# Expert attention: where DVE adds the fc2 bias, before or after a row's closing steps

## The chip, the cores and the metric

The kernel runs on one NeuronCore of a Trainium2 chip. Its time is the device time of one execution, in microseconds, and of several runs the median is compared. The engines are TensorE (PE; its weight loads are PEld), VectorE (DVE), ScalarE (ACT), GpSimd (POOL) and SyncE (SP), which only issues DMAs.

## The reference

The reference is a small audio network: a strided depthwise convolution, an ALiBi attention, the expert attention of this change, a Taylor-series attention and a mixture of experts. `h` has 32 batch rows of 188 positions and 64 channels. The part that matters (NH = 4 heads, NE = 4 query sets, called experts, D = 16):

```python
sx = einsum("bsh,ndh->bnsd", x, hl_w) + hl_b
q, k, v = per expert and head, per head, per head          # from sx
att = softmax(causal(q @ k.T * d ** 0.5))                  # one for each head and expert
qkv = where(pad, 0, att @ v)                               # "the mask"
gs = softmax(gate logits of qkv)                           # over the experts
hn = layernorm(sum over experts of qkv * gs + resid)
fx = hn by heads
hx = relu(where(fx == 0, 0, fx @ fc1_w.T + fc1_b))
hx = where(fx == 0, 0, hx @ fc2_w.T + fc2_b)               # "+ fc2_b" is the step that moves
fout = layernorm(hx + fx)
fg = softmax(fout @ fgate_w.T)
h = h + fout * fg                                          # "the closing steps"
```

## The kernel before, in words

The activations of all rows stay in SBUF, in the tensor `stream`; weights lie in `wsb`. `expert_attention` (from line 778) works as a software pipeline with one turn for each batch row. Each of the four engines runs its own `body(t, par)`, written out by hand, and in turn `t` each works on eight rows at once, at lags 0 to 7: LN, FRONT, UNIT, TAIL, NORM, MLP, FIN and LAST. In the code of a turn `rf`, `ru`, `rt`, `rz`, `rm`, `rn` and `rl` are these rows. `skewed_loop` (line 1452) writes out the first turns (the pipeline fills), loops over pairs of turns, and writes out the last ones (it drains, turns 32 to 38). The order on each engine is the order of the code. Waits between engines are semaphores named after the tile.

TensorE splits a turn into four steps `e`, one for each query set. In each it does the scores of that set (L1064, L1067, into PSUM banks `T`), the shifted queries of the next (L1041 to L1046), the maxima scores two sets ahead (L1028 to L1035, into `R`) and the weighing of the values of the set before (L1081, L1085, into `O`). Between these stand 14 small products, all of which use one PSUM bank, `X`, in the fixed order of the list `FILLS` (all at L993). Each must wait until the engine that reads the one before has said `..._used`:

```python
FILLS = [("znT", MLP), ("fg", LAST), ("sx", FRONT),
         ("pickA", TAIL), ("kb01", FRONT), ("kb23", FRONT), ("q01", FRONT),
         ("pickB", TAIL), ("fc1", MLP), ("k", FRONT),
         ("q23", FRONT), ("v", FRONT), ("xT", LN), ("fc2", MLP)]
```

`fc2` is the last product of a turn (behind the weighing of step 3). The next turn starts with the scores of set 0, and then come the transposes `znT`, which overwrite `X` and so wait for `fc2_used`. That semaphore is set by DVE's `hx = X + fc2_b` (L1376). After `znT` follow queries, `fg` (the gate product, read by DVE at L1281 and L1282, which frees the bank), maxima scores, the weighing of set 3, `sx`, and in step 1 the scores, `pickA`, queries and `kb01`. `pickA` waits for ACT's copies `sxT` and `sxb` (L1159). ACT overwrites `sxT` only after DVE's mask of set 3 of the row two before (`need(act, sem["o_used"], ...)`). `kb01` waits for DVE's `outs` (L1264).

DVE's turn begins with the sum over the experts (L1274, which waits for POOL's `mixed`, L967), the MLP's mask (L1277), the gate's maximum (L1281, L1282), additions to `z` (L1289, L1291), the maxima of set 2 (L1245, L1248) and the mask of set 3 (L1254). It ends with the maxima of set 1 of the next row, the gate of the experts (L1360 to L1362), the mask of set 2 (L1254), then the closing steps of row `rl` (L1368, L1369, L1370, L1371, L1373: sum, reciprocal, the gate, the product, the addition to `stream`; each waits for the one before through `link`), and last the bias of row `rm` (L1376). The closing steps exist in turns 7 to 38 and the bias in turns 5 to 36. POOL computes `mixed` (two instructions) at the turn's end, then zeroes the part above the diagonal of the exponentials (L979). In the first turns TensorE has one extra group of 16 matmuls per entry of `WARM_AT`, the last of them in turn 6 (just ahead of the stretch from 676 us that the rows below show).

Of the kernel before, what the change touches and what calls it, by code (L numbers as in the profile page):

```python
# [20 lines left out]
ALU = mybir.AluOpType  # L21
# [3 lines left out]
B, T_IN, C = 32, 375, 64  # L25
# [3 lines left out]
P = N // 2  # L29
HALVES = 2  # L30
# [335 lines left out]
class Steps:  # L366
# [12 lines left out]
    def link(self, ins):  # L379
        self.mark(ins)  # L380
        self.settle()
# [396 lines left out]
def expert_attention(env):  # L778
# [14 lines left out]
    with ExitStack() as ctx:  # L793
        def sb(name, shape, dt=F32):
            return ctx.enter_context(nc.sbuf_tensor("ex_" + name, shape, dt))
# [4 lines left out]
        def psum(name, shape):  # L800
            return ctx.enter_context(nc.psum_tensor("ex_" + name, shape, F32))
# [43 lines left out]
        hx = sb("hx", [P, HALVES, C])  # L845
# [8 lines left out]
        X = psum("X", [128, 512])  # L854
# [6 lines left out]
        sem = {n: ctx.enter_context(nc.semaphore("ex_" + n)) for n in names}  # L861
# [4 lines left out]
        def valid(r):  # L866
            return not isinstance(r, int) or 0 <= r < B

        def row_halves(r):
            return stream[:, bass.ds(r * HALVES, HALVES), :]  # L870

        def over_halves(name):
            return w(name, P).unsqueeze(1).broadcast_to([P, HALVES, w(name, P).shape[1]])

        def heads(t):

            return t.rearrange("p h (n d) -> p h n d", n=NH)
# [349 lines left out]
        def _(dve):  # L1227
            steps = Steps(dve, sem["dve_step"])
            link = steps.link
            tt, ts, red = nc.vector.tensor_tensor, nc.vector.tensor_scalar, nc.vector.tensor_reduce  # L1230
# [20 lines left out]
            def mask_values(r, e, par):  # L1251

                dve.wait_ge(sem["o_full"], r * NE + e + 1)
                nc.vector.scalar_tensor_tensor(oT[par][:, e, :], sxT[par][:, 0:N], 0.0, O[:, 0:N], ALU.not_equal,  # L1254
                                               ALU.mult).then_inc(sem["o_used"], 1)
# [11 lines left out]
            def body(t, par):  # L1267
                rf, ru, rt, rz, rm, rn, rl = (t - lag for lag in (FRONT, UNIT, TAIL, NORM, MLP, FIN, LAST))
# [94 lines left out]
                       top[:].unsqueeze(2).broadcast_to([P, HALVES * NH, NE]), ALU.mult).then_inc(sem["gs_ready"], 1)  # L1363
                if valid(ru):
                    mask_values(ru, 2, par)
                if valid(rl):
                    dve.wait_ge(sem["fexp_ready"], rl + 1)
                    link(red(fsum[:], fexp[:], AX.X, ALU.add))  # L1368
                    link(nc.vector.reciprocal(fsum[:], fsum[:]))  # L1369
                    link(tt(fexp[:], fexp[:], fsum[:].unsqueeze(2).broadcast_to([P, HALVES, NH]), ALU.mult))  # L1370
                    link(tt(heads(fout[:]), heads(zn[odd][:, :, 1, :]), fexp[:].unsqueeze(3)  # L1371
                            .broadcast_to([P, HALVES, NH, D]), ALU.mult))
                    link(tt(row_halves(rl), row_halves(rl), fout[:], ALU.add))  # L1373
                if valid(rm):
                    dve.wait_ge(sem["fc2_full"], rm + 1)
                    tt(hx[:], X[0:P, 0:HALVES * C].rearrange("p (h c) -> p h c", h=HALVES), over_halves("fc2_b"), ALU.add)\  # L1376
                        .then_inc(sem["fc2_used"], 1)

            dve.wait_ge(sem["consts"], CONSTS)
            skewed_loop(dve, body, DEPTH, steps, 2 * STEPS)  # L1380


# [812 lines left out]
```

## Time and profile before

| | us |
|---|---|
| median of 3 runs | 2023.95 (2016.03 to 2024.33) |
| the profiled execution, its own time | 2016.92 |
| its span, first to last instruction | 2015.0 |
| busy in the span: TensorE / its weight loads | 1701.8 / 1243.2 |
| busy in the span: DVE / ACT / POOL | 1382.7 / 768.3 / 595.6 |
| mean granted TensorE clock | 0.795 |

Times are microseconds from the start of the span. A row of a timeline is a run of like instructions: start, length, engine, line, operation, what it writes and reads, the shape, how many, and in brackets how long the engine stood idle before it and for whom. The ends of matmuls are modelled. The granted clock is a share of full speed: 1.00 is 2.4 GHz, 0.50 is 1.2 GHz. The page's chain of waits covers only the end of the program here.

### The profile page before, as it was taken

Reading aid. Unit: us, or ns where it says so; the run is one execution under the profiler, and the core shown is the slowest. Engines: PE = TensorE matmul, PEld = TensorE weight load, DVE = VectorE, ACT = ScalarE, POOL = GpSimd, SP = SyncE. Lnnn points to the kernel's source line nnn. Section 1 sums busy time; section 2 is a strip of 40 time slices with the busy share of each in tenths; the row PEclk is TensorE's granted clock in tenths of the full one; section 3 lists DMA queues with packets and bytes.
Section 4 is the critical chain, followed back from the end, with each engine's and each line's share of the span. In section 5 each row is a group of like instructions: output and inputs, shape, how many; then the busy total and the mean of one; then the engine's idle time right before and its main releaser. Section 6 shows DMA issues by size and latency. Waiting matters only on the chain. (4 is left out here: it accounts for less than half of the span.)

```text
span 2015.0 us, 45178 instructions
## 1 busy us (share of the span) xinstructions
PE 1701.8 (84%) x15237; PEld 1243.2 (62%) x15240; DVE 1382.7 (69%) x4295; ACT 768.3 (38%) x2210; POOL 595.6 (30%) x906
## 2 busy tenths in 40 slices
PE   1499999999769899999999999962999999788897
PEld 1266666666535556565555555541888888677776
DVE  6276766666527777777777777774766665688887
ACT  2255444454334444444444444421222222344443
POOL 2522222222134433333333333332211211322221
PEclk9999999999879977777777777765555555687888
DMA  2000000000000000000000000000000000000000
GB/s 114 1 2 0 0 0 0 0 0 0 1 1 2 2 1 0 0 0 0 0 0 0 0 0 0 0 1 0 1 0 0 0 0 1 1 5 6 5 4 13
DMA packets 6978, 8.12 MB, mean 4 GB/s; under 512 B 6272, under 2 KB 6272, under 8 KB 6784
## 3 DMA queue, kind: packets, MB, share of 16 engines
q1 hardware_dynamic: 6912, 7.25, 1.1%
q8 instruction: 40, 0.66, 0.1%
q14 instruction: 26, 0.21, 0.0%
HBM read 5.71 MB, written 1.54 MB: 4 GB/s over the span
## 5 line engine op out<-in xcount | busy, mean ns | idle before, releaser
L604 ACT ACTIVATE al_prob<-al_S,al_negmax 94x94 f32<-94x94 f32 (+1 forms) x512 | 145.9, 376 | 176.2 <-DVE al_negmax L731 176.1
L979 POOL TENSOR_SCALAR_AFFINE_SELECT ex_pT<-ex_pT 128x512 f32<-128x512 f32 (+1 forms) x256 | 129.3, 528 | 246.6 <-ACT ex_pT L1196 195.1
L505 PE MATMUL al_S<-al_kpad,al_qT 128*94 128x376 f32 x384 | 163.0, 507 | 0.0
L1245 DVE TENSOR_REDUCE ex_negmaxA<-ex_R 128x4 bf16<-128x512 f32 x128 | 88.9, 694 | 80.4 <-PE ex_R L1029 78.7
L682 POOL TENSOR_TENSOR al_kpad<-al_kT,al_quad_mask 128x1504 f32<-128x1504 f32 x32 | 86.2, 2694 | 183.7 <-ACTq L619 183.7
L731 DVE TENSOR_REDUCE al_negmax<-al_S 94x2 f32<-94x376 f32 (+1 forms) x192 | 99.2, 542 | 58.4 <-PE al_S L506 52.5
L1595 POOL TENSOR_TENSOR ta_kk<-ta_ext 94x320 f32<-94x320 f32 x64 | 60.4, 962 | 246.2 <-DVE ta_qkn L1775 166.1
L961 POOL TENSOR_TENSOR ex_zrstd<-ex_zvar,neg_half 94x16 f32<-94x16 f32 x34 | 98.6, 2901 | 77.1 <-DVE ex_zvar L1320 77.1
L1170 ACT ACTIVATE ex_pT<-ex_T 128x496 f32<-128x496 f32 x128 | 74.8, 584 | 92.8 <-PE ex_T L1067 92.7
L741 DVE RECIPROCAL al_rec<-al_O 128x188 f32<-128x188 f32 x64 | 84.9, 1327 | 32.1 <-PE al_O L543 32.1
L2004 ACT ACTIVATE mo_hT<-mo_H,wsb 128x188 f32<-128x188 f32 x256 | 88.4, 416 | 38.8 <-PE mo_H L1964 36.2
L1964 PE MATMUL mo_H<-mo_xT,w_parts 128*128 128x188 bf16 x768 | 93.7, 283 | 9.2 <-ACT mo_hT L2004 9.2
L1940 PE MATMUL mo_Y<-wsb,mo_hT 128*94 128x64 f32 x1024 | 100.4, 261 | 0.0
L1940 PEld LDWEIGHTS mo_Y<-wsb,mo_hT 128*94 128x94 f32 x1024 | 97.3, 177 | 0.3 <-issue 0.2
L993 PE MATMUL ex_X<-ident,ex_zn 94*128 94x94 f32 x136 | 32.5, 381 | 71.1 <-DVE ex_hx L1376 63.6
L1064 PE MATMUL ex_T<-ex_qm,ex_kT 32*128 32x188 f32 x1024 | 90.8, 417 | 0.9
L1964 PEld LDWEIGHTS mo_H<-mo_xT,w_parts 128*128 128x128 bf16 x768 | 73.3, 113 | 22.3 <-ACT mo_hT L2004 20.8
L1041 PE MATMUL ex_T<-ex_sxT,wsb 128*128 128x188 f32 x256 | 84.4, 419 | 0.0
L505 PEld LDWEIGHTS al_S<-al_kpad,al_qT 128*94 128x94 f32 x384 | 59.3, 168 | 39.1 <-issue 38.7
L993 PE MATMUL ex_X<-wsb,ex_oT 128*94 128x84 f32 x512 | 76.8, 311 | 5.2 <-ACT ex_sxb L1159 3.7
L737 DVE COPY al_probT<-al_PT 94x752 f32<-94x752 f32 x64 | 59.5, 930 | 29.5 <-PE al_PT L523 29.5
L967 POOL TENSOR_TENSOR ex_mixed<-ex_outs,ex_gate 94x256 f32<-94x256 f32 x64 | 39.5, 636 | 136.1 <-DVE ex_gate L1362 136.1
(321 smaller groups left out, 4471.2 us busy)
## 6 DMA issues: line engine op xcount, KB each, us to landing
tok_xin<-x_t SPq DMA_DIRECT2D x4, 760.0 KB, 7.2
wsb<-weights SPq DMA_DIRECT2D x1, 2531.0 KB, 13.9
out<-stream SPq DMA_DIRECT2D x16, 94.0 KB
tok_par<-tok_w SPq DMA_DIRECT2D x1, 4.5 KB, 1.6
```

The source lines that it names most:

```text
L505: nc.tensor.matmul(S[0:P, k, 0:2 * N], q, s, start=True, stop=False)
L604: last = nc.scalar.activation(p[:, k, cols], S[0:P, k, cols], ACT.Exp, bias=negmax[g % 2][:, m:m + 1])
L682: nc.gpsimd.tensor_tensor(kpad[par][:].rearrange("p j g n -> p j (g n)"), kT[:].rearrange("p g n -> p (g n)").unsqueeze(1).broadcast_to([1 ...
L731: nc.vector.tensor_reduce(dst, src, AX.X, ALU.max, negate=True).then_inc(max_done, 1)
L961: nc.gpsimd.tensor_tensor(zrstd[:], zvar[:], neg_half[0:P, 0:HALVES * 2 * NH], ALU.pow)\
L979: nc.gpsimd.affine_select(out=view, in_=view, compare_op=ALU.is_ge, fill=0.0, base=shift, pattern=[[0, NH], [1, cols]], channel_multiplier ...
L993: last = nc.tensor.matmul(dst, a, m, start=True, stop=True)
L1064: last = nc.tensor.matmul(T[:, n, 0:N], kT[par][rows, 0:K0], qm[e % 2][rows, :], start=True, stop=True, tile_position=(32 * n, 0), skip_gr ...
L1245: red(negmaxA[e % 2][:, D::32], R[:, 0, :].rearrange("p (n s) -> p n s", n=NH), AX.X, ALU.max, negate=True)\
L1940: last = nc.tensor.matmul(YB[h][0:P, e * C:(e + 1) * C], hT[p][:, e, h * P:(h + 1) * P], w("w2")[:, e * C:(e + 1) * C], start=True, stop=True)
L1964: last = nc.tensor.matmul(HB[e // 2 % 2][:, (e % 2) * N:(e % 2 + 1) * N], w_parts[:, b, e * HID:(e + 1) * HID], xT[p][:, a, :], start=(n = ...
L2004: nc.scalar.activation(hT[p][:, e, :], HB[e // 2 % 2][:, (e % 2) * N:(e % 2 + 1) * N], ACT.Gelu, bias=w("b1")[:, e:e + 1]).then_inc(h_read ...
```

## The change

On DVE, the block with the wait for `fc2_full` and the bias goes from the end of the turn to just behind the mask of set 2. Nothing else is changed: the same instructions, semaphores and operands.

```diff
                 if valid(ru):
                     mask_values(ru, 2, par)
+                if valid(rm):
+                    dve.wait_ge(sem["fc2_full"], rm + 1)
+                    tt(hx[:], X[0:P, 0:HALVES * C].rearrange("p (h c) -> p h c", h=HALVES), over_halves("fc2_b"), ALU.add)\
+                        .then_inc(sem["fc2_used"], 1)
                 if valid(rl):
                     dve.wait_ge(sem["fexp_ready"], rl + 1)
                     link(red(fsum[:], fexp[:], AX.X, ALU.add))
                     link(nc.vector.reciprocal(fsum[:], fsum[:]))
                     link(tt(fexp[:], fexp[:], fsum[:].unsqueeze(2).broadcast_to([P, HALVES, NH]), ALU.mult))
                     link(tt(heads(fout[:]), heads(zn[odd][:, :, 1, :]), fexp[:].unsqueeze(3)
                             .broadcast_to([P, HALVES, NH, D]), ALU.mult))
                     link(tt(row_halves(rl), row_halves(rl), fout[:], ALU.add))
-                if valid(rm):
-                    dve.wait_ge(sem["fc2_full"], rm + 1)
-                    tt(hx[:], X[0:P, 0:HALVES * C].rearrange("p (h c) -> p h c", h=HALVES), over_halves("fc2_b"), ALU.add)\
-                        .then_inc(sem["fc2_used"], 1)
```

## Rows read from the trace of the kernel before

**Rows 1.** The page's slices of the span (50.4 us each): TensorE's granted clock, in tenths

```profile
PEclk9999999999879977777777777765555555687888
```

**Rows 2.** Waits of the stage, 566 to 1392 us: in total, times, longest

```profile
PE ex_X L993 <- DVE ex_hx L1376: 63.6, 30, 4.9
```

**Rows 3.** DVE's timeline, one steady row: start, length, line, [idle before]

```profile
1019.30 0.15 DVE L1368 TENSOR_REDUCE ex_fsum<-ex_fexp 94x2 f32<-94x8 f32 x1
...
1019.68 0.76 DVE L1370 TENSOR_TENSOR ex_fexp<-ex_fexp,ex_fsum 94x8 f32<-94x8 f32 x1
...
1021.64 0.29 DVE L1376 TENSOR_TENSOR ex_hx<-ex_X,wsb 94x128 f32<-94x128 f32 x1
```

**Rows 4.** TensorE's timeline, the same row

```profile
1018.90 0.54 PE L993 MATMUL ex_X<-wsb,ex_h1m 64*94 64x64 f32 x4
...
1022.08 0.65 PE L993 MATMUL ex_X<-ident,ex_zn 94*128 94x94 f32 x4 [1.92 <-DVE ex_hx L1376]
...
1023.81 0.59 PE L1028 MATMUL ex_R<-ex_kpadb,ex_qTb 128*128 128x512 bf16 x1
...
1026.56 0.99 PE L993 MATMUL ex_X<-ex_xT,wsb 64*128 64x188 f32 x2
...
1028.75 1.57 PE L993 MATMUL ex_X<-wsb,ex_oT 128*94 128x84 f32 x8
```

**Rows 5.** Stretches: length, each engine's busy time, granted clock, DMA share, GB/s

```profile
677.10:696.91 19.81, 17.62 (x218) 11.64 (x218) 15.98 (x49) 10.09 (x26) 8.84 (x14) 1.00 0.01 2
...
724.74:1318.63 593.89, 536.92 (x5228) 349.33 (x5228) 432.14 (x1290) 245.17 (x623) 215.52 (x310) 0.78 0.00 0
...
995.63:1009.28 13.65, 12.70 (x82) 7.91 (x82) 8.05 (x24) 4.24 (x11) 3.14 (x7) 0.50 0.00 0
...
1022.92:1033.16 10.24, 10.05 (x67) 6.04 (x66) 5.52 (x20) 3.67 (x10) 2.07 (x5) 0.50 0.00 0
...
193.49:196.91 3.42, 3.42 (x8) 1.54 (x7) 1.12 (x3) 1.54 (x7) 0.00 (x0) 0.50 0.00 0
```

**Rows 6.** TensorE's timeline, turns 6 and 7, at full clock

```profile
679.15 0.38 PE L1028 MATMUL ex_R<-ex_kpadb,ex_qTb 128*128 128x512 bf16 x1
...
680.81 0.58 PE L993 MATMUL ex_X<-ex_xT,wsb 64*128 64x188 f32 x2
...
683.29 0.87 PE L993 MATMUL ex_X<-wsb,ex_oT 128*94 128x84 f32 x8 [1.19 <-ACT ex_sxb L1159]
...
685.25 0.32 PE L993 MATMUL ex_X<-ex_sxb,ex_ewkb 128*128 128x188 bf16 x2 [0.63 <-DVE ex_outs L1264]
...
699.55 0.74 PE L993 MATMUL ex_X<-ident,ex_zn 94*128 94x94 f32 x2 [1.84 <-DVE ex_hx L1376]
```

**Rows 7.** DVE's timeline, turns 6 and 7

```profile
676.71 0.34 DVE L1254 SCALAR_TENSOR_TENSOR ex_oT<-ex_sxT,ex_O 128x188 f32<-128x188 f32 x1
...
677.10 0.29 DVE L1376 TENSOR_TENSOR ex_hx<-ex_X,wsb 94x128 f32<-94x128 f32 x1
...
678.14 1.12 DVE L1274 TENSOR_REDUCE ex_z<-ex_mixed 94x64 f32<-94x256 f32 x2 [0.76 <-POOL ex_mixed L967]
...
681.99 0.33 DVE L1254 SCALAR_TENSOR_TENSOR ex_oT<-ex_sxT,ex_O 128x188 f32<-128x188 f32 x1
...
696.65 0.34 DVE L1254 SCALAR_TENSOR_TENSOR ex_oT<-ex_sxT,ex_O 128x188 f32<-128x188 f32 x1
```

**Rows 8.** ACT's timeline, turn 7

```profile
682.42 0.42 ACT L1159 ACTIVATE ex_sxT<-ex_X,wsb 128x188 f32<-128x188 f32 x1 [2.74 <-DVE ex_oT L1254]
```

**Rows 9.** POOL's timeline, the steady row of rows 3

```profile
1019.18 1.24 POOL L967 TENSOR_TENSOR ex_mixed<-ex_outs,ex_gate 94x256 f32<-94x256 f32 x2 [4.10 <-DVE ex_gate L1362]
```

**Rows 10.** The bias in the steady rows: durations, first and last start

```profile
L1376 DVE TENSOR_TENSOR ex_hx<-ex_X,wsb x25: 286/286/288, 724.7 to 1318.6; 94x128 f32<-94x128 f32 x25
```

**Rows 11.** DVE's timeline, a draining turn

```profile
1366.96 0.16 DVE L1370 TENSOR_TENSOR ex_fexp<-ex_fexp,ex_fsum 94x8 f32<-94x8 f32 x1
...
1370.62 0.16 DVE L1281 TENSOR_REDUCE ex_ftop<-ex_X 94x2 f32<-94x8 f32 x1 [2.21 <-PE ex_X L993]
```

## The prediction

> **What bounds the kernel now.** I read the page first, for where the time lies and what clock it had; then the waits of the stage of the expert attention, for what TensorE waits on; then the timelines of TensorE and DVE across one steady row; then the same two timelines across the one row that ran at full clock without closing steps; last the stretches with their granted clock.
>
> The expert attention's rows run from about 566 to 1392 us. TensorE's granted clock has a 9 in the two slices from 604 to 705 and a 7 in every one of the twelve behind them, the steady rows [rows 1]. The largest wait of TensorE in the stage is for `hx`, the very instruction that the change moves: 63.6 us in 30 rows, 2.1 each, one in each turn in which both a bias and closing steps exist (turns 7 to 36) [rows 2]. In the steady row shown, DVE starts the first closing step at 1019.30, right behind the row's last mask. L1370 alone takes 0.76. The bias starts at 1021.64, so the closing steps hold it back by 2.34 us [rows 3]. The matmul that it reads (fc2) ended at 1018.90 + 0.54 = 1019.44. TensorE, which runs in order, ends its scores about 1020.15 and stands idle for 1.92 us until the transposes of `zn` can overwrite `X` at 1022.08 [rows 4]. So the bias could have run from about 1019.5 to 1019.8, before TensorE wanted the bank.
>
> The second reading is the clock. It fell to 0.50 (1.2 GHz) at 1022.92, behind that gap, and was back at 1.00 (2.4 GHz) at 1033.16; the stretch before, from 995.63 to 1009.28, was the same thing one row earlier. Over the 24 steady periods the mean is 0.78, so 0.44 of the time, 10.9 us of a row, runs at half clock [rows 5]. At half clock the maxima matmuls and the weighing, up to the start of `sx`, take 1023.81 to 1026.56 = 2.75 us [rows 4]; at full clock the same matmuls take 679.15 to 680.81 = 1.66 us [rows 6]. A microsecond of gapless work at half clock is thus 0.60 of one at full clock and loses 0.40.
>
> **The change, step by step.** No instruction is added or removed, and none issues a DMA. On DVE the 0.29 us bias with its wait for fc2 goes ahead of five closing steps. No queue of POOL, ACT or SP is reordered.
>
> *Gap at znT.* Gone at both clocks: TensorE reaches the transposes about 0.35 us after the bias could end. In turn 6, where there are no closing steps, the mask starts at 676.71, the bias at 677.10 [rows 7], and TensorE never waited between scores and transposes. Nearest bounds for the new wait for fc2, behind which the closing steps are now queued: 0 (turn 6) to the 0.14 by which fc2's end at 1019.44 lies behind 1019.30 [rows 3, 4]; I take 0.1.
>
> *What is late next.* The closing steps still stand before the next turn's work on DVE, and its mask of the last query set (L1254) gates ACT's copies of `sxT` and `sxb`, then `pickA`, then `kb01`. Turn 6 into 7 shows that chain at full clock: the mask starts at 681.99, ACT waited 2.74 us for it and starts at 682.42 [rows 7, 8]; `pickA` starts at 683.29 after TensorE idled 1.19, `kb01` at 685.25 after 0.63 more for `outs` [rows 6]. From there TensorE is dense until the next fc2. That turn's whole period, mask to mask, is 696.65 - 676.71 = 19.94 us at clock 1.00 [rows 5, 7]. Adding closing steps in its place behind the bias moves the mask. Raw, they are 2.34 long; 0.76 of that falls into DVE's wait for POOL's `mixed` at 678.14 [rows 7], plus some 0.1 of wait for fc2: 19.94 + 1.6 = 21.5. But L1370 is not 0.76 long by itself. Without POOL beside it, it is 0.16 [rows 11]; in the steady row it ends at 1019.68 + 0.76 = 1020.44, just as `mixed` ends at 1019.18 + 1.24 = 1020.42 [rows 3, 9]. Started 0.4 later it should end at the same moment, so I take off the 0.4 that bias and wait cost: a mask 1.1 later, a period of **21.05 us** at full clock. Bounds 20.4 (closing steps shrink to their unheld length) and 21.6 (none of it absorbed).
>
> *The clock.* The idle piece at `pickA` grows from 1.19 to 1.19 + 1.1 = 2.3 us, longer than the 1.92 behind which the clock falls now; 1.19 with 0.63 behind it did not bring it down [rows 5, 6]. So I expect the clock to fall still, but at `pickA`, and to return sooner: in the steady row it was back at 1033.16, 4.4 us after `pickA` began at 1028.75 [rows 4, 5], because then the wide matmuls run. The shortest low stretch in the trace is 3.42 [rows 5], the longest 13.65. I take 4.5 us of low work, 0.40 x 4.5 = 1.8, in 8 rows of 10, since a gap of 2.3 sits near the boundary between what did and did not bring it down: 1.45 a row. Period 21.05 + 1.45 = **22.5**.
>
> The Trainium skill's page "TensorE: Matmul & The Clock Gate", section "HAM oscillation — how this bites in real kernels", prices throttled time at half of it, 1 - 1.2/2.4. By that the 4.5 us would cost 2.25, not 1.8, a row 22.85 and the whole 8 us more. No row here shows a full 0.5; the pair above measures 0.40 with its weight loads and small matmuls, and the measurement decides.
>
> *Sum.* Steady period now: (1318.6 - 724.7)/24 = 24.745 [rows 10]. 24 x (24.745 - 22.5) = 53.9. Turn 7 has one idle piece of 1.84 at the same place [rows 6]: 1.8. In the draining turns 33 to 36 TensorE has little to do and the chain bias, transposes, `fg`, L1281 is serial; DVE idles up to 2.21 at L1281 [rows 11], so 0 to 2.2 each, I take 1.25: 5. Together **61 us**. The profiled execution took 2016.92 (span 2015.0 and 1.9 around it), so 1956 on its scale; the median of the runs is 2023.95, 7 above it, and the forecast is made against that: **1963**.
>
> **The rivals.**
> - *The clock holds.* For it: two slices of this stage (604 to 705 us) have a 9 for the clock, in turns with gaps of 1.19 and 0.63 [rows 1, 6]. Against: the new gap is longer than the one that brings it down now. Period 21.05, 24 x 3.695 + 7 = 96 us less: **1928**.
> - *The clock falls at `pickA` and returns later*, after 7 us of low work: the row has 21.05 + 2.8 = 23.85; 24 x 0.9 + 7 = 28 less: **1996**. For it: the remaining wait at `kb01` still thins the work right behind.
> - *Slower: the low stretch keeps its length and lands on the dense part.* Now half of it lies between transposes and `kb01`, where TensorE has 1.19 + 0.63 = 1.8 us of slack at full clock anyway [rows 6]. From `pickA` on it has none. With stretches of 10.24 and 13.65 as now (mean 11.9) [rows 5], a row is 21.05 + 4.8 = 25.8, 24 x 1.06 - 7 = 18 more: **2042**. It turns from gain to loss at a low stretch of (24.745 + 0.29 - 21.05)/0.40 = 10 us. Against it: the return 4.4 us behind `pickA`.
> - *No difference:* the same stretch at 9 to 11 us, or fc2 so late that the closing steps lose what TensorE gains; within 10 us of **2024**.
>
> **How the numbers follow.** Forecast 0.52, clock holds 0.20, later return 0.15, no difference 0.06, slower 0.07. Two in ten may lie outside; 1925 to 2000 takes in the first three with their bounds (a period of 20.4 would reach 1913, unlikely). Faster by over 0.5% (10 us, about what a measurement of this kernel can tell): the first three, 0.87.
>
> **What would show it.** In the changed profile the row "TensorE waits for `hx`" should be nearly gone; L1254 and then the bias stand back to back, with L1370 shorter than 0.76; a wait of TensorE at `pickA` for ACT's `sxb` of about 2 us a row should be new; ACT's `sxT` should wait for `oT`. The mean clock of the steady rows should be 0.88 to 0.95. The forecast is wrong if the clock stays at 0.78 or lower, or is 1.00 throughout, or if the bias idles for fc2 by more than 0.3 us a row.

## The result, and the profile after

The changed kernel takes 1943.22 us (median of 4 runs, 1939.4 to 1945.91), the kernel before 2021.39 us (4 runs, 2016.03 to 2024.33). The ratio is 0.9615, 95% interval 0.9586 to 0.9644: 78 us faster. The forecast was 1963, with a range of 1925 to 2000. The profiled execution has a span of 1937.5 us, against 2015.0. Its page, busy time of three engines and TensorE's clock by slices (now 48.4 us each):

```profile
PE 1621.5 (84%) x15237; PEld 1186.3 (61%) x15240; DVE 1358.8 (70%) x4295; ACT 765.0 (39%) x2210; POOL 595.3 (31%) x906
...
PEclk9999999999969998889888888855555555897888
```

The same instructions ran. The slices of the steady rows had a 7 before [rows 1] and have mostly an 8 now. TensorE's busy time fell by 80 us with the same 15237 matmuls: they were shorter, not fewer. The waits of the stage (in total, times, longest), 566 to 1320 us:

```profile
ACT ex_sxT L1159 <- DVE ex_oT L1254: 95.1, 29, 3.6
...
PE ex_X L993 <- ACT ex_sxb L1159: 39.6, 31, 1.5
...
PE ex_X L993 <- DVE ex_hx L1368: 9.5, 4, 3.6
```

The wait for the bias, 63.6 us in 30 rows before [rows 2], is 9.5 us in 4 rows, all of them where the pipeline drains. In its place stands TensorE's wait for ACT's `sxb`, 1.3 us a row; ACT in turn waits for DVE's mask of set 3, 3.60 us in the row shown. That row on DVE, from the end of turn 21 into turn 22 (the counterpart of rows 3 and 7; `hx` is now at L1368 and the closing steps at L1372 to L1377):

```profile
1002.58 0.35 DVE L1254 SCALAR_TENSOR_TENSOR ex_oT<-ex_sxT,ex_O 128x188 f32<-128x188 f32 x1
...
1003.02 0.29 DVE L1368 TENSOR_TENSOR ex_hx<-ex_X,wsb 94x128 f32<-94x128 f32 x1
...
1003.60 0.37 DVE L1374 TENSOR_TENSOR ex_fexp<-ex_fexp,ex_fsum 94x8 f32<-94x8 f32 x1
...
1004.01 0.68 DVE L1375 TENSOR_TENSOR ex_fout<-ex_zn,ex_fexp 94x128 f32<-94x128 f32 x1
...
1005.68 1.12 DVE L1274 TENSOR_REDUCE ex_z<-ex_mixed 94x64 f32<-94x256 f32 x2 [0.55 <-DVE stream L1377]
...
1007.51 0.29 DVE L1289 TENSOR_TENSOR ex_z<-ex_z,residual 94x128 f32<-94x128 f32 x1 [0.15 <-DVE ex_fgate L1282]
...
1007.72 0.28 DVE L1291 TENSOR_TENSOR ex_z<-ex_hx,ex_zn 94x128 f32<-94x128 f32 x1
...
1008.98 0.34 DVE L1254 SCALAR_TENSOR_TENSOR ex_oT<-ex_sxT,ex_O 128x188 f32<-128x188 f32 x1
```

And on TensorE, the same row (the counterpart of rows 4 and 6):

```profile
1002.44 0.54 PE L993 MATMUL ex_X<-wsb,ex_h1m 64*94 64x64 f32 x4
...
1003.83 0.68 PE L993 MATMUL ex_X<-ident,ex_zn 94*128 94x94 f32 x4
...
1007.47 0.58 PE L993 MATMUL ex_X<-ex_xT,wsb 64*128 64x188 f32 x2 [0.46 <-DVEq L1285]
...
1010.19 1.57 PE L993 MATMUL ex_X<-wsb,ex_oT 128*94 128x84 f32 x8 [1.43 <-ACT ex_sxb L1159]
...
1012.86 0.47 PE L993 MATMUL ex_X<-ex_sxb,ex_ewkb 128*128 128x188 bf16 x2 [0.19 <-DVE ex_outs L1264]
```

The bias starts at 1003.02, right behind fc2's end at 1002.98. The transposes at 1003.83 follow the scores without an idle piece. `sx` waits 0.46 for DVE's reading of the gate, and `pickA` 1.43 (the next row has 0.27 and 1.36, and so on in turn; the piece at `pickA` is 1.40 on average). The clock over the 24 steady rows, over most of a low stretch (which lasts from 1009.33 to 1016.16), over the time behind it up to and into the next, and over a row that had no low stretch:

```profile
717.94:1250.92 532.98, 475.03 (x5238) 306.81 (x5242) 410.38 (x1291) 242.06 (x623) 215.28 (x311) 0.89 0.00 0
...
1010.15:1016.90 6.75, 6.52 (x48) 3.89 (x52) 3.28 (x10) 2.62 (x7) 1.81 (x4) 0.56 0.00 0
...
1017.00:1033.90 16.90, 14.90 (x183) 10.26 (x176) 14.29 (x48) 7.92 (x22) 8.11 (x11) 0.98 0.00 0
...
717.94:738.55 20.61, 17.78 (x218) 11.63 (x218) 17.21 (x54) 10.09 (x26) 9.08 (x14) 1.00 0.01 2
```

The clock still falls, in the idle piece ahead of `pickA` or shortly behind it, in 22 of the 24 rows. It is back after 3.4 us in twelve of them and after 6.8 in nine, where it took 10.2 or 13.7 [rows 5]. At half clock a row now spends 0.22 of 22.2 = 4.9 us, not 10.9.

Where the 77.5 us of span went, by the starts of the bias (turn 8 / turn 32 / turn 36): 724.7 / 1318.6 / 1379.3 before, 717.9 / 1250.9 / 1302.2 after. So 6.8 us were won up to turn 8, 593.9 - 533.0 = 60.9 in the 24 steady periods (24.745 to 22.208 us a row), 60.7 - 51.3 = 9.4 in the four turns where the pipeline drains, and 0.4 elsewhere.

### The profile page after: what moved, and what is told of

Same layout as the page of the kernel before. It is cut to its first block and busy times, and to the rows that moved or that the text cites. A ratio compares the mean times of both kernels' runs of the same rounds, so it can differ in the third digit from the quotient of the medians.

```text
span 1937.5 us, 45153 instructions
## 1 busy us (share of the span) xinstructions
PE 1621.5 (84%) x15237; PEld 1186.3 (61%) x15240; DVE 1358.8 (70%) x4295; ACT 765.0 (39%) x2210; POOL 595.3 (31%) x906
## 5 line engine op out<-in xcount | busy, mean ns | idle before, releaser
L979 POOL TENSOR_SCALAR_AFFINE_SELECT ex_pT<-ex_pT 128x512 f32<-128x512 f32 (+1 forms) x256 | 129.4, 529 | 154.0 <-ACT ex_pT L1196 140.6
L993 PE MATMUL ex_X<-wsb,ex_oT 128*94 128x84 f32 x512 | 68.9, 288 | 42.2 <-ACT ex_sxb L1159 38.7
L1940 PE MATMUL mo_Y<-wsb,mo_hT 128*94 128x64 f32 x1024 | 94.5, 252 | 0.0
L1940 PEld LDWEIGHTS mo_Y<-wsb,mo_hT 128*94 128x94 f32 x1024 | 91.4, 168 | 0.3 <-issue 0.2
L993 PEld LDWEIGHTS ex_X<-wsb,ex_oT 128*94 128x94 f32 x512 | 57.7, 192 | 48.7 <-ACT ex_sxb L1159 36.7
L1964 PEld LDWEIGHTS mo_H<-mo_xT,w_parts 128*128 128x128 bf16 x768 | 73.2, 112 | 22.1 <-ACT mo_hT L2004 20.9
L1064 PE MATMUL ex_T<-ex_qm,ex_kT 32*128 32x188 f32 x1024 | 80.2, 371 | 0.7 <-issue 0.2
L1041 PE MATMUL ex_T<-ex_sxT,wsb 128*128 128x188 f32 x256 | 74.9, 378 | 0.0
```

Source lines behind the costliest of these rows:

```text
L979: nc.gpsimd.affine_select(out=view, in_=view, compare_op=ALU.is_ge, fill=0.0, base=shift, pattern=[[0, NH], [1, cols]], channel_multiplier ...
L993: last = nc.tensor.matmul(dst, a, m, start=True, stop=True)
L1940: last = nc.tensor.matmul(YB[h][0:P, e * C:(e + 1) * C], hT[p][:, e, h * P:(h + 1) * P], w("w2")[:, e * C:(e + 1) * C], start=True, stop=True)
L1964: last = nc.tensor.matmul(HB[e // 2 % 2][:, (e % 2) * N:(e % 2 + 1) * N], w_parts[:, b, e * HID:(e + 1) * HID], xT[p][:, a, :], start=(n = ...
```

## The experiments

Two theories were set against each other. **A**: the idle piece costs twice, by its own length and by the clock that it brings down. **B**: only the idle time counts. "A row" is the mean period of the bias over the 24 steady rows. Four of the kernels have `bridge(n)`, a loop of n dummy matmuls on TensorE, into columns of `T` that nothing reads:

```python
def bridge(n):
    for _ in range(n):
        nc.tensor.matmul(T[:, 1, 256:512], w_parts[:, 0, 0:128], w_parts[:, 0, 128:384], start=True,
                         stop=True, skip_group_check=True)
```

### The kernel before, with its idle piece filled

```diff
+                    if e == 0 and valid(rl) and valid(rm) and valid(ru):
+                        bridge(14)
                     if e == 0 and valid2(rm):
                         pe.wait_ge(sem["zn_ready"], rm + 1)
```

> The kernel before, with 14 dummy matmuls (256 columns, about 0.11 us each at full clock, 1.55 us together) in TensorE's queue just ahead of the transposes of zn, in the turns that have both a bias and closing steps. They fill the idle piece of 1.92 us and delay nothing. Theory A (the idle piece costs twice: itself, and the clock it brings down): the mean clock of the steady rows goes from 0.78 to about 1.00, a row from 24.75 to 22.1 us, as turn 6 to 7 had it at full clock; 24 x 2.6 = 62 us less than before, about 1960. Theory B (only the idle time itself counts, the clock's fall is a by-product worth little): no change, 2021 within 5. Theory C (the clock falls for another reason than this idle piece): clock stays at 0.78 and the time at 2021 or above.

Measured: 1959.1 us, ratio 0.9701 (0.9679 to 0.9723). The bias is where it was and DVE does what it did; TensorE was only given useless work to do while it waits. The bias in the steady rows (durations, first and last start), and the stretch's clock:

```profile
L1384 DVE TENSOR_TENSOR ex_hx<-ex_X,wsb x25: 286/286/288, 727.6 to 1269.5; 94x128 f32<-94x128 f32 x25
```

```profile
727.50:1270.00 542.50, 491.39 (x5568) 329.57 (x5565) 432.85 (x1293) 242.36 (x623) 215.70 (x310) 0.95 0.00 0
```

A row takes 22.58 us at a mean clock of 0.95. Theory B, which expected 2021, falls, and so does C, the thought that the clock fell for another reason. The clock alone was worth over 2 us a row. The time is what A expected, but its row of 22.1 us at clock 1.00 was not reached: this kernel has idle pieces of 1.09 us at `pickA` too, behind which the clock fell in 10 of the 24 rows. These rows give the clock's price: one without a low stretch takes 21.8 us, one with 3.4 us at half clock 22.8, one with 10.2 us 25.7. That is 0.28 to 0.38 us lost for each microsecond at half clock. In no run do the dummies stand where TensorE isn't waiting. That they act by filling this wait, and not simply as more work in the row, is therefore argued (the clock now falls only behind the piece at `pickA`, where this kernel has no dummies) and not shown apart.

### The changed kernel, with the new idle piece filled

```diff
+                    if e == 1 and valid(rl) and valid(rt):
+                        bridge(10)
                     if e == 1 and valid(rt):
                         pe.wait_ge(sem["o_used"], NE * (rt + 1))
```

> The changed kernel, with 10 of the same dummy matmuls (1.1 us) ahead of pickA, where TensorE now idles 1.43 us for ACT's sxb, in the turns with closing steps. Theory A: the clock of the steady rows goes from 0.89 to about 1.00, a row from 22.2 to 20.6 us (what the changed kernel's own row at clock 1.00 takes, 717.94 to 738.55); 24 x 1.6 = 38 less, about 1905. Theory B: no change, 1943 within 5. If the dummies end behind the moment at which sxb is ready, up to 0.3 a row is given back, about 1912.

Measured: 1904.84 us, ratio 0.9436 (0.9415 to 0.9457).

```profile
L1376 DVE TENSOR_TENSOR ex_hx<-ex_X,wsb x25: 280/287/288, 718.5 to 1215.5; 94x128 f32<-94x128 f32 x25
```

```profile
718.00:1216.00 498.00, 459.44 (x5493) 305.46 (x5490) 411.27 (x1295) 241.86 (x624) 215.63 (x312) 1.00 0.00 0
```

A row takes 20.71 us at clock 1.00, and the time is what A expected to within a microsecond. What the changed kernel still pays for the clock is 22.21 - 20.71 = 1.50 us a row.

### Four dummies instead of ten

The same edit with `bridge(4)`.

> The changed kernel with 4 dummy matmuls (0.44 us) instead of 10 ahead of pickA. They are issued in the same place and cost TensorE's queue less. The idle piece there should be about 1.0 instead of 1.43 (0.2 with ten). Theory A with a soft boundary: the clock falls in some rows only; between 1905 and 1943, about 1920. If what counts is that the dummies are there at all: 1905. If the boundary lies below 1.0 us of idle time: about 1940.

Measured: 1907.87 us, ratio 0.9448 (0.9429 to 0.9467). TensorE still waits for `sxb`, 0.85 us a row instead of 1.40, and the clock fell in two of the 24 rows.

```profile
PE ex_X L993 <- ACT ex_sxb L1167: 20.5, 24, 0.9
```

```profile
719.50:1219.00 499.50, 446.04 (x5342) 293.20 (x5340) 410.75 (x1292) 241.76 (x623) 215.05 (x311) 0.99 0.00 0
```

The expected 1920 was too high. Within the noise the time is that of ten dummies, 1904.84. That fits two readings: an idle piece of 0.85 us costs almost nothing here, or it counts that there are dummies at all, the expectation's rival of 1905. This run does not tell them apart. In the kernel above and in others further down, pieces of 1.09 us without a dummy at `pickA` are followed by a fall in many rows.

### The bias halfway through the closing steps

```diff
-                bias
                 if valid(rl):
                     (sum, reciprocal, gate)
+                bias
                     (product, addition to stream)
```

> The changed kernel, but with the bias behind the first three closing steps (sum, reciprocal, gate) and ahead of the last two. The bias then starts 0.7 to 1.1 us later than in the changed kernel, 1.2 to 1.6 earlier than before; TensorE should idle 0.3 to 0.7 at the transposes. Theory A (the clock makes it a threshold): an idle piece that short does not bring the clock down there, a row is 0.3 to 0.7 longer than the changed kernel's, 1950 to 1960. Theory B (proportional to the idle piece): 0.5 of 1.92 gives 0.26 of the 78 us back, 1963. Should the clock fall twice in a row (here and at pickA), it would be 1985 or more.

Measured: 1960.63 us, ratio 0.9708 (0.9678 to 0.9738). The time lies at A's upper end and at B's value, so it does not tell them apart. The trace shows what A had wrong in it. The idle piece at the transposes of one steady row, with the clock in front of it and behind it, and the piece of the next row:

```profile
930.95 0.68 PE L993 MATMUL ex_X<-ident,ex_zn 94*128 94x94 f32 x4 [0.45 <-DVE ex_hx L1373]
```

```profile
928.95:932.40 3.45, 2.96 (x40) 2.50 (x34) 2.61 (x10) 1.18 (x4) 2.23 (x4) 0.98 0.00 0
932.40:942.60 10.20, 10.01 (x67) 5.68 (x71) 6.79 (x22) 3.31 (x10) 2.75 (x6) 0.51 0.00 0
```

```profile
954.35 0.65 PE L993 MATMUL ex_X<-ident,ex_zn 94*128 94x94 f32 x4 [0.75 <-DVE ex_hx L1373]
```

An idle piece of only 0.45 us at the transposes was followed by 10 us at half clock, in seven rows of this kernel. The longer pieces of 0.75 at the same place, in the rows between, were not: there the clock was still up when TensorE began to wait at `pickA`, and in the row shown it stayed up to the row's end, 20.67 us at 1.00. Only in the last steady row did it fall right behind such a piece. So neither the length of a piece nor its place decides alone whether the clock falls, and the threshold in A's expectation is wrong. What else decides stays open. The row took 22.64 us on average, with a mean clock of 0.87.

### The bias later than before

```diff
+                if valid(rn):
+                    dve.wait_ge(sem["fc2_full"], rn + 1)
+                    (bias)
                 if valid(rn):
                     dve.wait_ge(sem["fc2_used"], rn + 1)
```

> The kernel before, with the bias held back further: it goes into the next turn, behind the sum over the experts (L1274, 1.1 us) and just ahead of its reader. The idle piece of TensorE at the transposes should grow from 1.92 to about 3.0 us. Theory A (the piece has already brought the clock down; a longer one costs its own length, less what TensorE catches up while DVE's chain is the later one): a row 0.9 to 1.3 us longer, 2019 + 22 to 31 = 2041 to 2050, mean clock 0.74 to 0.80. Theory B (the idle time alone, 78 us for 1.92): 1.1 more is 45 us, 2064. If nothing but the clock mattered: 2019.

Measured: 2078.34 us against 2019.75, ratio 1.0286 (1.0267 to 1.0305).

```profile
PE ex_X L993 <- DVE ex_hx L1277: 72.9, 24, 3.1
```

```profile
738.50:1376.00 637.50, 549.68 (x5228) 357.40 (x5228) 434.99 (x1292) 244.84 (x623) 214.85 (x310) 0.75 0.00 0
```

The idle piece is the 3.0 us that was expected. In the kernel before it is 1.92 in one half of the steady rows and about 1.57 in the other, 1.76 on average, so the wait grew by 1.3 us a row and not by 1.1. The cost, 59 us, is above both theories: A said 22 to 31, B 45. A row is 26.55, so 1.80 longer; 43 of the 59 are there. Of the rest, 14 us lie in the turns up to 8, which also have the bias, and little where the pipeline drains. The mean clock went down from 0.78 to 0.75; the low stretches added up, which is finer than the rounded clock, are 13.0 us a row instead of 11.1. At 0.40 a microsecond that is 0.8 us more, with which the row would be 2.1 longer; that slack took the other 0.3 is an inference. A's price of "its own length only" had left the clock's part out.

### The closing steps in the middle of the turn

```diff
                 if valid(rt):
                     pick_heads(rt, 0, "pickA")
+                (the five closing steps)
                 if valid(ru):
                     maxima(ru, 3)
```

> The changed kernel, with the five closing steps moved from the end of the turn to the middle, ahead of the maxima of set 3, where DVE waits 0.94 us for TensorE at full clock. The mask of set 3, which gates ACT's sxT and TensorE's pickA, then comes some 2 us earlier in the turn. Theory A: the wait at pickA is back at 1.2 us or less, the clock stays at 1.00 as in turns 6 and 7 of the kernel before, and a row takes 20.0 to 20.4 us, the closing steps' remaining 1.4 us on DVE being mostly hidden: 24 x 2.0 = 48 less, about 1895. Theory B (no part of the clock in it): the row loses only the longer wait at pickA, 0.7 us, 1925. Rival D (DVE is by now what bounds a row): no gain, 1943, since DVE has the same work.

Measured: 1920.35 us (1909.32 to 1929.77), ratio 0.9494 (0.9458 to 0.9529). Rival D falls: DVE does not bound the row. The fastest rows take 19.87 us, but the mean is 21.41, at clock 0.91. The piece at `pickA` is 1.08 us on average, and behind it the clock still fell in 16 of the 24 rows, for 3.4 or 10.2 us:

```profile
PE ex_X L993 <- ACT ex_sxb L1159: 26.0, 24, 1.2
```

```profile
723.00:1237.20 514.20, 469.03 (x5246) 307.06 (x5245) 406.94 (x1292) 241.76 (x623) 214.55 (x311) 0.91 0.00 0
```

The runs scatter widely, and the clock with them: the slowest, 1929.77 us, which is the profiled one, had a mean granted clock of 0.836 over its whole span, the fastest, 1909.32, had 0.846. The expected 1895 supposed that a piece under 1.2 us leaves the clock up, as one row of the kernel before had it [rows 6]; that supposition was wrong.

### The same, with the piece at `pickA` filled

`bridge(8)` ahead of `pickA`, on the kernel of the last section.

> The kernel with the closing steps in the middle of the turn, with 8 dummy matmuls (0.88 us) ahead of pickA, where TensorE idles 1.09 us. Theory A: the clock stays at 1.00 and every row takes what that kernel's fast rows take, 19.87 to 20.13: against its mean of 21.41 that is 24 x 1.4 = 34 less than 1920, about 1888. Rival D (DVE bounds the row now): 1905, as the changed kernel with its clock held. If the remaining wait of 0.6 for outs is enough to bring the clock down in some rows: 1895 to 1910.

Measured: 1895.12 us (1891.44 to 1896.26), ratio 0.9376 (0.936 to 0.9392). This is the fastest version, 48 us below the changed kernel.

```profile
L1384 DVE TENSOR_TENSOR ex_hx<-ex_X,wsb x25: 278/287/288, 722.0 to 1201.2; 94x128 f32<-94x128 f32 x25
```

```profile
722.00:1201.50 479.50, 452.15 (x5437) 300.29 (x5436) 401.65 (x1291) 241.75 (x623) 214.15 (x311) 1.00 0.00 0
```

A row takes 19.97 us, at clock 1.00, as A expected. The time is 7 us above the 1888 that was expected for it, because that took the row's gain, read from the profiled run of 1929.77, off the median of 1920. The 0.63 us idle piece that remains at `kb01` brought nothing down.

### Without the closing steps

The five closing steps are left out of the changed kernel, so the result of this attention is never added to `stream`; the count of DVE's steps in a turn goes down with them.

> The changed kernel without the five closing steps at all (so the result of this attention is not added to the stream; everything else runs). It bounds what the steps still cost where the change has put the bias. By turn 6 into 7 of the kernel before, a row then takes 19.94 us at full clock, with an idle piece of 1.2 at pickA behind which the clock falls in some rows, as it did with the closing steps in the middle: 20.9 to 21.4 a row, 1905 to 1920. If the clock is held by the shorter piece: 1888. If the closing steps cost nothing any more: 1943.

Measured: 1910.19 us (1903.89 to 1916.62), ratio 0.9467 (0.9439 to 0.9496).

```profile
720.50:1219.70 499.20, 453.69 (x5248) 300.06 (x5246) 387.25 (x1172) 242.08 (x623) 214.85 (x311) 0.94 0.00 0
```

In the profiled run, the fastest of the four, a row is 20.78 at clock 0.94; behind the piece of 1.09 us at `pickA` the clock fell in 12 of the 24 rows. The closing steps thus still cost the changed kernel 33 us where they stand. Of the 1.43 us that its row is longer, 0.7 are there at full clock too (20.7 against 20.0, the mean of this kernel's rows of 19.87 and 20.1), and the rest is the clock. Moved to the middle of the turn they cost 10 (1920 against 1910), which is inside the two kernels' scatter; at full clock the rows of both take 19.9 and 20.1.

### Without POOL's zeroing

POOL's zeroing above the diagonal (L979) is left out of the changed kernel, so later keys keep their weight; its semaphore is counted up all the same.

> The changed kernel with POOL's zeroing above the diagonal (L979) left out: the later keys keep their weights, and the semaphore is counted up in its place. It asks whether the long forms of four DVE instructions with two SBUF inputs (product L1375 0.68 us, gate L1374 0.37, and before the change L1289 0.62 and L1291 0.47) come from POOL's work beside them. If so: L1375 falls to 0.29 and L1289 and L1291 stay at 0.29 and 0.28; L1374 stays at 0.37, since beside it runs POOL's mixed product, which is left in. The mask of set 3 comes 0.4 us earlier, the idle piece at pickA shrinks from 1.43 to about 1.0, the clock falls in fewer rows, and the time is 1905 to 1925. If the long form of L1375 has another cause: it stays at 0.68, and the time at 1935 to 1945, unless the weighing, which waits for the zeroing, was late.

Measured: 1938.68 us (2 runs), ratio 0.9594 (0.9566 to 0.9622). DVE's gate and product, in this kernel at L1372 and L1373:

```profile
1009.81 0.37 DVE L1372 TENSOR_TENSOR ex_fexp<-ex_fexp,ex_fsum 94x8 f32<-94x8 f32 x1
1010.21 0.29 DVE L1373 TENSOR_TENSOR ex_fout<-ex_zn,ex_fexp 94x128 f32<-94x128 f32 x1
```

The product goes from 0.68 to 0.29 us with POOL's work beside it gone, and the gate, beside POOL's `mixed`, stays at 0.37, as expected. The time was not what the expectation gave with it, 1905 to 1925. The 0.39 us that the product gave back went into TensorE's wait at `sx`, 0.37 a row in the changed kernel and gone here; the idle piece at `pickA` is 1.34 on average, against 1.40. Rows of 20.44 us at full clock alternate with rows of 23.93, and in each of those the clock is low for 10.2 us. A pair of them:

```profile
1015.88 0.90 PE L991 MATMUL ex_X<-wsb,ex_oT 128*94 128x84 f32 x8 [1.43 <-ACT ex_sxb L1157]
...
1035.92 1.57 PE L991 MATMUL ex_X<-wsb,ex_oT 128*94 128x84 f32 x8 [1.25 <-ACT ex_sxb L1157]
```

```profile
1009.22:1029.66 20.44, 18.01 (x222) 11.96 (x222) 16.35 (x54) 10.10 (x26) 5.06 (x6) 1.00 0.00 0
1029.66:1053.59 23.93, 22.08 (x218) 14.47 (x218) 16.55 (x54) 10.08 (x26) 5.02 (x6) 0.79 0.00 0
```

The row with the longer piece, 1.43 us, kept its clock, and the one with 1.25 lost it: again the length does not decide alone. A row is 22.31 against 22.21, with 5.6 us of it at half clock on average against 4.8 (low stretches added up), so the clock took back what the product had given.

## Why the prediction was right

- *Gap at znT.* As predicted, the idle piece is gone, with no new wait for fc2 that shows. It was 1.92 us in only every second steady row, the one that the prediction read; in the others it was about 1.57. fc2's end and the bias's start are 0.04 us apart.
- *What is late next.* As predicted: mask of set 3, ACT's `sxT` and `sxb` (waited for 3.60 us), `pickA`. The idle piece there is 1.43 us where 2.3 was forecast, since 0.46 of the delay is taken earlier, at `sx`. The mask of set 3 starts 6.40 us behind the mask of set 2 in the row shown and 5.91 in the next; the forecast's 5.28 + 1.1 fits the first and is 0.5 too late for the second.
- *The full-clock period* was the mis-sized term: 21.05 forecast, 20.6 measured (the row from 717.94 to 738.55) and 20.71 as a mean with the clock held, where rows of 20.99 and 20.45 take turns. The gate's shortening (0.76 to 0.37) was in the forecast. Not in it: L1289 and L1291 took 0.62 and 0.47 us in the steady rows before and take 0.29 and 0.28 now, 0.52 together, and both lie on the way to the mask. In the other direction 0.55 us of idling on DVE ahead of L1274, in every second turn, now lies on that way too. Every second turn ends a pass of DVE's loop, so it is likely the loop's end; no run shows that apart.
- *The clock.* 1.45 us a row forecast, 1.50 measured. The place (`pickA`), the earlier return and the mean clock (0.88 to 0.95 forecast, 0.89 measured) came out. That the two sizes lie so close is luck, two errors that cancel. The price of 0.40 per microsecond was near for the long stretches and too high for the short ones (0.38 and 0.28 in the first experiment); a longer time at half clock made up for it, 4.9 us a row where 3.6 was assumed (4.5 in eight rows of ten; 22 of 24 fell). The page "TensorE: Matmul & The Clock Gate" of the Trainium skill, section "HAM oscillation — how this bites in real kernels", prices each throttled microsecond at half of one; the measured 4.9 us cost 1.50, so 0.31 each, and the trace doesn't agree. The reason given for the fall, a piece longer than 1.92, was wrong: the piece was 1.40, and pieces of 1.09, shorter than the 1.19 that had left the clock up [rows 6], were followed by a fall in 10, 16 and 12 of 24 rows of three kernels. Nor does any run show that the wide matmuls bring the clock back: behind the same `pickA`, in the kernel with the closing steps in the middle of the turn, it stayed low for 3.4 us in some rows and for 10.2 in others. And 13.65 is the longest low stretch of the steady rows only; from 1340 us on the kernel before stood at half clock for 403 us.
- *The sum.* 61 us forecast, 78 measured. 7 of the 17 missing are in the steady rows (22.5 against 22.21). 5 are in the first periods: I counted only turn 7's idle piece and 24 periods, and left out that turn 7 to 8, 25.53 us before, gets shorter as well (20.78). 4.4 are in the draining turns, 9.4 against 5. The median came out 20 below the forecast and not 17, because that of the kernel before is 2021.39 in the result, 2.6 less than what the forecast was set against.
- *The rivals.* "The clock holds" did not come true by itself, but the kernel with ten dummies is that case: 1905, where this rival had 1928. "Later return" describes nine of the 24 rows, with 6.8 us at half clock, but these took 22.5 to 23.0 us and not 23.85. "Slower" had the long stretch behind `pickA`, and one row in 24 shows it: from 1186.8 the clock was low for 13.7 us, and that row took 25.94.

How the steady row's 2.54 us divide: with the bias late, a row at full clock takes 21.8 (the filled kernel before, in its rows without a low stretch); with it early, 20.7 (the filled changed kernel). So 1.1 us is order alone, and the other 1.4 is the clock, which cost 24.75 - 21.8 = 2.9 us a row before and costs 1.5 now. That is worked out from two kernels with dummy work in them. What makes the clock fall behind one idle piece and not behind the next of the same length, in the same place, stays open. The fills show only that without these pieces it did not fall in any steady row: in the two kernels whose piece at `pickA` was filled to under 0.3 us, all 24 rows stood at 1.00.

## What to carry to other kernels

Where an engine in order waits for a short instruction that stands behind a longer chain on its own engine, and nobody waits for that chain, put the short one first; then ask what the chain is now ahead of. An idle piece of TensorE is to be priced with the clock behind it: look at the granted clock in the 10 us after it, and try the fill with dummy matmuls, which costs three lines and tells the clock's share apart from the wait's. Such a fill was worth 38 us on top of the change, and the move of the chain into a wait that DVE has in the middle of its turn 10 more.

## What the runs showed of the hardware

A 0.45 us idle piece of TensorE among small matmuls (transposes, scores of 32 rows, fc2) was followed by 10 us at 1.2 GHz, while one of 0.75 us at the same place, in the next row of the same kernel, was not. Ahead of `pickA` a piece of 1.25 us was followed by 10.2 us at 1.2 GHz and one of 1.43 by none, again in one kernel. With ten or eight dummy matmuls into unused columns of a PSUM bank ahead of `pickA` the clock stayed at 1.00 in all 24 steady rows.

DVE's product of two SBUF tensors (94 x 128, f32) took 0.68 us beside POOL's zeroing and 0.29 without it. The Trainium skill's page "SBUF — State Buffer", section "Who interferes with whom", says that a DVE instruction with two SBUF inputs contends with a GpSimd instruction that reads SBUF; the trace agrees, 0.68 against 0.29 us. The bias, with one input in PSUM, took 0.28 to 0.29 us in every row, with POOL's `mixed` running beside it (the changed kernel, from 1003.02) or not (the kernel before, from 1021.64).
